# Causal select on GpSimd, exponent-bit rounding and a reordered opening in a four-layer gated-attention kernel

## The reference, cut to what matters

```python
for l in range(4):
    x = x + tanh(g_xattn[l]) * attention[l](layernorm(x), ctx)
    x = x + tanh(g_ffn[l]) * ffn[l](layernorm(x))
# attention 2: a query sees the keys up to its own place
scores = einsum('bhqd,bhkd->bhqk', Q, K) / sqrt(8)
scores = where(tril(ones), scores, -inf)
attn = softmax(scores)
# ffn 3: blocks of 32 are divided by max|block| / 7.5, rounded to the grid
# +-(m/8, or (1+m/8)*2^(e-1)), 0..7.5, ties to the lower value, and multiplied back
out = quantised(x) @ quantised(weight).T + bias
```

## Time and profile before

| | |
|---|---|
| three runs | 963.58, 964.5, 966.36 us; median 964.5 |
| the profiled execution | 962.56 us, its span 960.8 us |
| mean granted TensorE clock | 0.963 of full speed |
| TensorE busy | 883.2 us, 92% |
| VectorE / ScalarE / GpSimd busy | 74% / 66% / 48% |

### The profile page before, as it was taken

How to read it: one execution, slowest core, us unless ns; L and a number is a source line. 1 busy time by engine, 2 the same in 40 slices (tenths; PEclk the granted TensorE clock), 3 DMA queues, 4 the chain that set the end, 5 groups by cost and what they waited for, 6 DMA issues and landing times.

```text
span 960.8 us, 22930 instructions
## 1 busy us (share of the span) xinstructions
PE 883.2 (92%) x8153; PEld 614.4 (64%) x8153; DVE 707.6 (74%) x2203; ACT 638.1 (66%) x1463; POOL 457.2 (48%) x563
## 2 busy tenths in 40 slices
PE   4797889999999999999987899999999999999973
PEld 2343446866799987478443365767679987887432
DVE  4898997768452378987998999798754257747987
ACT  1587667676876436796664777777787557777751
POOL 5527554862851134545356265555642514612362
PEclk7799999999999999999998999999999999999975
DMA  6523242221110010002102020120110100000000
GB/s 161 127 59 100 53 121 53 77 64 37 28 45 1 17 34 3 20 26 65 33 20 73 20 71 23 36 53 19 37 36 1 30 23 18 14 23 2 21 2 23
DMA packets 67664, 40.06 MB, mean 42 GB/s; under 512 B 8279, under 2 KB 65520, under 8 KB 67552
## 3 DMA queue, kind: packets, MB, share of 16 engines
q1 hardware_dynamic: 61056, 28.93, 11.6%
q0 software_dynamic: 2208, 6.78, 2.6%
q10 hardware_dynamic: 4288, 2.87, 1.3%
HBM read 11.19 MB, written 1.05 MB: 13 GB/s over the span
## 4 chain that ended last, share of the span: by engine, by line
PE 74%; DVE 11%; ACT 5%; POOL 5%; issue 3%; DMA 2%; ACTq 1%; SPq 0%; DVEq 0%; POOLq 0%
PE banks L1065 13%; PE banks L1056 13%; PE banks L889 9%; PE banks L1025 7%; PE banks L865 5%; PE banks L842 5%; PE banks L828 4%; PE banks L1035 4%; DVE mx L1372 3%; PE banks L821 3%; POOL h L596 3%; PE banks L994 2%; ACT probs L735 2%; PE banks L934 2%; PE banks L850 1%
## 5 line engine op out<-in xcount | busy, mean ns | idle before, releaser
L1372 DVE TENSOR_REDUCE mx<-banks 128x4 f32<-128x1024 f32 (+1 forms) x240 | 284.3, 1217 | 29.6 <-PE banks L842 22.1
L735 ACT ACTIVATE probs<-banks 128x512 f32<-128x512 f32 (+1 forms) x512 | 258.3, 581 | 55.1 <-PE banks L865 35.7
L793 ACT ACTIVATE probs<-banks,b_sb 128x256 f32<-128x256 f32 x288 | 117.4, 472 | 71.4 <-PE banks L1056 69.8
L889 PE MATMUL banks<-probs,v_aug 128*9 128x256 f32 (+1 forms) x2048 | 151.1, 378 | 7.2 <-ACT probs L735 6.3
L589 POOL TENSOR_TENSOR rstd<-veps,mhalf 128x2 f32<-128x2 f32 x64 | 46.2, 722 | 197.9 <-DVE veps L1321 197.2
L1065 PE MATMUL banks<-w_sb,probs 128*128 128x128 f32 x1152 | 139.9, 276 | 0.0
L1065 PEld LDWEIGHTS banks<-w_sb,probs 128*128 128x128 f32 x1152 | 135.6, 192 | 4.7 <-issue 2.1
L1056 PE MATMUL banks<-hT,w_sb 128*128 128x256 f32 x576 | 137.1, 382 | 0.0
L637 POOL TENSOR_TENSOR rn<-ss,mhalf 128x32 f32<-128x32 f32 x16 | 87.9, 5497 | 77.8 <-DVE ss L1168 77.8
L1056 PEld LDWEIGHTS banks<-hT,w_sb 128*128 128x128 f32 x576 | 104.3, 190 | 13.6 <-issue 0.8
L1244 DVE SCALAR_TENSOR_TENSOR xs<-banks,comb,xs 128x128 f32<-128x128 f32 x144 | 43.7, 345 | 91.9 <-PE banks L1065 87.2
(11 more groups left out here) (203 smaller groups left out, 1476.8 us busy)
## 6 DMA issues: line engine op xcount, KB each, us to landing
k_st<-k_parts SPq DMA_DIRECT2D x186, 64.0 KB, 2.0
q_st<-q_parts SPq DMA_DIRECT2D x186, 64.0 KB, 2.1
w_sb<-in_w POOLq DMA_DIRECT2D x16, 256.0 KB, 3.4
fc_sb<-in_fc POOLq DMA_DIRECT2D x6, 256.0 KB, 3.9
x_in<-in_x SPq DMA_DIRECT2D x8, 128.0 KB, 3.6
cT<-in_ctxT SPq DMA_DIRECT2D x8, 128.0 KB, 3.1
out_x<-xs SPq DMA_DIRECT2D x8, 128.0 KB, 1.9
q_st<-mT SPq DMA_DIRECT2D x32, 16.0 KB
```

Source lines behind the costliest of these rows:

```text
L735: nc.scalar.activation(probs[s][:, part % UNIT_RING, 2 * a:2 * a + 2, 0:n], b_bank(w, a + 1)[:, 0:2 * n].rearrange("p (j q) -> p j q", j=2 ...
L793: ins = nc.scalar.activation(hid[s][:, part % UNIT_RING, c, :], b_bank(w, half + 1)[:, j * ROWS:(j + 1) * ROWS], ACT.Gelu, bias=b1_sb[:, p ...
L889: ins = nc.tensor.matmul(c_bank(b, l, u // 4)[VW * i:VW * i + VR, g % 2, q0:ROWS], v_aug[s][:, t, 4 * g + i, :], probs[s][:, u % UNIT_RING ...
L1372: nc.vector.tensor_reduce(mx[s][:, r, :, hp0:hp0 + n], banks[:, first:first + 2, :].rearrange("p a (n k) -> p a n k", n=n), AX.X, ALU.max) ...
```

## The change

1. **Causal mask of the turned scores.** The four matmuls of each unit (L870 to L878) go. GpSimd gets one `affine_select` per unit on `probs`, in place, over four heads times the 128 queries of the diagonal block, after the exponentials; `weigh` waits for it. The row-wise mask (L850) stays. `ckq`, its load and its cast go.
2. **Rounding.** Part 4 takes the exponent bits of y with a bitwise and on VectorE, in place of ScalarE's square; eight parts (4 to 11) with one VectorE instruction each follow the division, then the multiplication back as part 12.
3. **Opening.** VectorE clears slot 0 first, makes the first statistics, then copies the weights by heads; slot 3 is cleared after the first norm. ScalarE evaluates one tanh on one element ahead of everything and the gates after the first keys. Of the `attention_loads`, two small ones are issued by ScalarE at the start, the three large ones by SyncE after the second tile of maxima of stream 0. K's first-term moves of streams 0 and 1 go to SyncE's queue. The `setup` parts stand among the maxima of stream 0 (places 4, 7, 9, 11). `late_loads` move from step 50 to 80.
4. **Order.** `TURNS_TAKEN` and `BANKS_TAKEN` are new. Stream 0's query now comes before stream 1's keys, stream 0's maxima before stream 2's norm. In layer 2 the mean distance between a unit's `attend` and its `weigh` is 12.2 steps where it was 10.3; elsewhere the order of the steps is close to the former one.

```diff
-MAGIC = 1.5 * 2.0 ** 23
+MAGIC = 1.5 * 2.0 ** 20
+EXPONENT = 0x7F800000
-ROW_PARTS, KEY_ROW_PARTS, FP6_PARTS, ... = 5, 3, 14, 4, 4
+ROW_PARTS, KEY_ROW_PARTS, FP6_PARTS, ... = 5, 3, 13, 4, 4
-BLK_AT, ..., LATE_AT = 90, 110, 9, 230, 12, 50
+BLK_AT, ..., LATE_AT = 90, 110, 9, 230, 12, 80
...
# stream_steps
-        out += [("setup", 0, part) for part in range(SETUP_PARTS)] * (l == 0)
+        if l == 0:
+            for part, place in enumerate((4, 7, 9, 11)):
+                tiles.insert(place, ("setup", 0, part))
...
# sync
-                    if b >= SPLIT_STREAMS or l > 0:
+                    if step == "keys" or b >= SPLIT_STREAMS or l > 0:
...
+                if (step, b, l, part) == ("maxima", 0, 0, 1):
+                    for dst, src in attention_loads[EARLY_LOADS:]:
+                        sp.dma_start(dst, src).then_inc(attn_loaded, 16)
...
# gpsimd
+                if step == "attend" and l == CAUSAL:
+                    pool.wait_ge(sems["b_read"], w.at("b_read", 2))
+                    seen = probs[s][:, part % UNIT_RING, :, 0:P]
+                    nc.gpsimd.affine_select(seen, seen, [[0, 4], [1, P]], ALU.is_ge, 0.0, base=0, channel_multiplier=-1)\
+                        .then_inc(sems["causal_ready"], 1)
...
# scalar
+            for dst, src in attention_loads[:EARLY_LOADS]:
+                act.dma_start(dst, src).then_inc(attn_loaded, 16)
+            act.wait_ge(zeros_ready, 1)
+            nc.scalar.activation(warm[:, :], mhalf[0:1, 0:1], ACT.Tanh)
...
-                    if b < SPLIT_STREAMS and l == 0:
+                    if step == "query" and b < SPLIT_STREAMS and l == 0:
...
-                if step == "query" and (b, l) == (0, 0):
+                if (step, b, l) == ("keys", 0, 0):
                     act.wait_ge(gates_loaded, 16 * len(gate_loads))
                     nc.scalar.activation(tg[:, :], gates[:, :], ACT.Tanh).then_inc(gates_done, 1)
...
-                if step == "quantise" and part == 4:
-                    nc.scalar.activation(work_rows[1][s][:, :, :], work_rows[0][s][:, :, :], ACT.Square)\
...
# tensor: the mask's matmuls in scores_turned go; weigh:
+                if l == CAUSAL:
+                    pe.wait_ge(sems["causal_ready"], w.at_step("causal_ready", 1, "attend", b, l, u))
+                else:
+                    pe.wait_ge(sems["b_read"], w.at_step("b_read", 2, "attend", b, l, u))
...
# vector
+            clear_keys(nc.vector, 0, cleared_dve)
-            dve.wait_ge(weights_loaded, 16 * len(weight_loads))
-            split_heads(0).then_inc(first_ready, 1)
...
                 if part == 4:
+                    return nc.vector.tensor_scalar(a.bitcast(U32), y.bitcast(U32), EXPONENT, None, ALU.bitwise_and)
                 if part == 5:
+                    return nc.vector.tensor_scalar(m2, a, 1.0, MAGIC, ALU.max, ALU.mult)
                 if part == 6:
+                    return nc.vector.tensor_tensor(inv, y, m2, ALU.add)
                 if part == 7:
+                    return nc.vector.tensor_tensor(inv, inv, m2, ALU.subtract)
                 if part == 8:
+                    return nc.vector.tensor_tensor(y, inv, y, ALU.subtract)
                 if part == 9:
+                    return nc.vector.scalar_tensor_tensor(a, y, 16.0 * MAGIC, m2, ALU.mult, ALU.is_ge)
                 if part == 10:
+                    return nc.vector.tensor_tensor(a, a, m2, ALU.mult)
                 if part == 11:
+                    return nc.vector.scalar_tensor_tensor(y, a, -0.125 / MAGIC, inv, ALU.mult, ALU.add)
...
                     if (b, l) == (0, 0):
-                        clear_keys(nc.vector, 0, cleared_dve)
-                        clear_queries(nc.vector, 3)
-                        clear_keys(nc.vector, 3, cleared_dve)
+                        dve.wait_ge(weights_loaded, 16 * len(weight_loads))
+                        split_heads(0).then_inc(first_ready, 1)
...
+                    if b == 0:
+                        clear_queries(nc.vector, 3)
+                        clear_keys(nc.vector, 3, cleared_dve)
```

More of the change, by code:

```diff
@@ L351, in flamingo @@
         ident = sb("ident", [P, P])
-        mask_b = sb("mask_b", [P, 3, P], BF16)
-        mask_swapped = sb("mask_swapped", [P, 3, P], BF16)
-        identb, cqk_b, ckq_b = (mask_b[:, i, :] for i in range(3))
+        mask_b = sb("mask_b", [P, 2, P], BF16)
+        mask_swapped = sb("mask_swapped", [P, 2, P], BF16)
+        identb, cqk_b = (mask_b[:, i, :] for i in range(2))
         before = sb("before", [P, RT, ROWS], BF16)
@@ L425, in flamingo @@
         before_f = spare[:, 2 * D:6 * D].rearrange("p (t k) -> p t k", t=RT)
-        cqk, ckq = (spare[:, i * D:(i + 1) * D] for i in range(2))
+        cqk = spare[:, 0:D]
         w3_sb = work_rows[0][0][:, 1, :]
@@ L697, in _ @@
                                          bias=bcol[:, l, c:c + 1]).then_inc(sems["b_read"], 1)
-                    if b < SPLIT_STREAMS and l == 0:
-                        name, terms, st = ("k", K_TERMS, k_st[s]) if step == "keys" else ("q", Q_TERMS, q_st[s])
+                    if step == "query" and b < SPLIT_STREAMS and l == 0:
                         act.wait_ge(*CLEARED[s])
                         act.wait_ge(sems[f"hi_ready{s}"], w.at(f"hi_ready{s}", 1))
-                        move_parts(act, terms, 0, st, parts[s], sems[f"{name}_moved{s}"])
-                if step == "query" and (b, l) == (0, 0):
+                        move_parts(act, Q_TERMS, 0, q_st[s], parts[s], sems[f"q_moved{s}"])
+                if (step, b, l) == ("keys", 0, 0):
                     act.wait_ge(gates_loaded, 16 * len(gate_loads))
                     nc.scalar.activation(tg[:, :], gates[:, :], ACT.Tanh).then_inc(gates_done, 1)
-                    for dst, src in attention_loads[:EARLY_LOADS]:
-                        act.dma_start(dst, src).then_inc(attn_loaded, 16)
-                if (step, b, l) == ("keys", 1, 0) and STEP["keys", 1, 0, 0] < STEP["setup", 0, 0, 0]:
-                    for dst, src in attention_loads[EARLY_LOADS:]:
-                        act.dma_start(dst, src).then_inc(attn_loaded, 16)
                 if w.i == LATE_AT:
@@ L1503, in _ @@
                     accumulate(s, lambda r: comb[s][:, r, part:part + 1])
-                if step == "quantise" and part not in (3, 4, FP6_PARTS - 1):
+                if step == "quantise" and part not in (3, FP6_PARTS - 1):
                     if part == 0:
                         dve.wait_ge(sems[f"h_ready{s}"], w.at_step(f"h_ready{s}", 1, "norm", b, 2 * LAYERS - 1, 0))
-                    elif part == 5:
-                        dve.wait_ge(sems["fp6_squared"], w.at_step("fp6_squared", 1, "quantise", b, l, 4))
+                    elif part == 4:
+                        dve.wait_ge(sems["fp6_divided"], w.at_step("fp6_divided", 1, "quantise", b, l, 3))
                     else:
```

132 lines of the change are left out of this document (52 added, 80 removed).

## The result

The changed kernel takes 959.43 us (median of 22 runs, 954.34 to 964.91) where the kernel before took 964.36 beside it (22 runs): ratio 0.9955, 95% interval 0.9943 to 0.9966. It is faster, by 4.9 us between the medians and 4.3 us by the ratio; 18 were forecast. The time lies inside the range given, 933 to 960, by 0.6 us.

What follows compares the result with a forecast made beforehand. Limits differed: TensorE in masked stretches, VectorE from 24 to 120 and 470 to 560 us, nothing full in the first 24. Gains 6.1 + 7.5 + 2 + 2.5 = 18.1 us gave 946.4 us, range 933 to 960.

Steps and rivals of the forecast that it cites:

- the pricing of the new order at nothing: Order of steps: no term of its own in the sum, only more steps between `attend` and `weigh`, 12.2 against 10.3.
- the opening: First 24 us: first scores at about 16 us, nine earlier, of which 7.5 us gained, ends 3 and 10.
- rounding and end: Rounding of streams 0 to 2, 2 us, ends 0 and 4.8; last stream's end, 2.5 us, ends 1 and 3.5.
- the mask: Layer 2's masked stretches: TensorE loses 13.9 us of work, selects cost GpSimd 1.0 us each; 6.1 us gained.
- (a): Masked waves: GpSimd late with a select at 1.34 us, opening at its lower end; 956.5, up to 964.5 us; 15%.
- (d): Opening: comes no earlier because first scores wait for a landing as now; 10.6 us gained, 953.9 us; 10%.
- case (c): Mask: select as cheap as a copy, TensorE's whole 13.9 us come back; 25.8 us gained in all, 938.7 us; 20%.
- The arithmetic of GpSimd's capacity: Masked waves: GpSimd's work summed per window; mask gains 13.8 us at 0.7 us a select, loses 4.0 at 1.34.
- The wait behind the norm: GpSimd's queue: 12.2 steps cover 1 us of latency, not a select behind a 5.45 us norm of heads; no size given.
- Rival (b): Masked waves: slower, select costs 3.25 us like a per-partition tensor_scalar; 66 us more, 1031 us; 9%.
- The prediction's measure: Opening: VectorE's idle time before 24 us counts; 12.3 us falls to 6 with scores at 16 us.
- the prediction's own last check: Opening: if first scores come at 16 us but VectorE idles as much before 60 us, the shift was absorbed.

Runs made afterwards that it cites:

- the two variants: Kernel before with the GpSimd select alone, ratio 1.0428; and all parts of the change with the select, former order after step 40, ratio 1.0453.
- the opening alone: Kernel before with the reordered start of every queue and the new steps up to stream 0's first attend, mask and rounding as before: ratio 0.9985.
- doubled selects: Changed kernel with every select of the probabilities issued twice in a row: ratio 1.0081 to the kernel before.

## Why the prediction was wrong

**The failed step is the pricing of the new order at nothing, and with it the sum itself.** The forecast took four terms, each read from the kernel before, and added them as if the order of steps were given. Measured in the former order, where they were read, they are worth far less: the opening 6.1 us less than its term, rounding and end 4.0, the mask 2.1 even with a select that costs nothing, and together they give 4.9 of the 18.1. In the new order they are worth about what was forecast or more, but there they only make up for an order that loses 20 us without them. That the time lies inside the range is no merit of the sum: it lies 0.6 us from the upper end, which was set by rivals (a) and (d).

| term | forecast, us | former order | new order |
|---|---|---|---|
| opening | 7.5 | 1.4 | 5.4 |
| mask by select | 6.1 | 4.0 (no select at all) | 8.7 |
| rounding and end | 4.5 | 0.5 | 14 to 15 |
| new order, former parts | 0 | | -20 |
| the select, against no select | (in the mask's) | -45 to -49 | 0 |
| together, measured | 18.1 | 4.9 without the select | 4.3 |

The new order's column adds up to 8 or 9, not 4.3. Its errors, about 2 us for each term, may cover that, and parts that are taken out one at a time need not add up: opening and rounding are 19.7 to 20.3 us one by one and 16.0 together. With the 16.0 the column closes: -20.3 + 16.0 + 8.7 = 4.4. Why the new order loses 20 us under the former ones was not tried further, and stays open.

**Mask.** The amount removed was right to the row: 64 units, 0.217 us. The select was priced at 1.0 us and takes 0.64; the bound from the nearest one-input rows was the better guide. By the Trainium skill's GPSIMD Engine Reference ("Performance pitfalls for Q7 kernels") the estimate was 0.44 or 0.87 us plus dispatch; the 64 selects lie between the two at 0.64, and nothing here shows the branching price of 5.1 us that its cycle accounting would give. What failed is case (c)'s condition, a cheap select, as the thing that decides. It holds, and still less than half of 13.8 us came in the former order. The windows showed TensorE at 99% of these stretches, and I took that for a distance to the next limit. It is none: of the 13.9 us taken away 4.0 came in the former order and 8.7 in the new one, and then other waits hold the time. Of these only VectorE's maxima were tried, 3.1 us for half of their work in layer 2. Rival (a) had the number, 956.5 and up to 964.5, and not the mechanism: its select of 1.34 us would hold up the waves, and here TensorE waits 2.6 us for all selects. The arithmetic of GpSimd's capacity came near in size and by another road: for 1.34 us a select it gave 17.8 us more than for a cheap one, and 1.28 us measured 12 more. It went by the sums of whole windows, while in the trace the sum of the first wave fits (35.1 of 40 us) and the queueing sits in its last ten microseconds.

**The wait behind the norm.** The prediction named it: 12.2 steps cover a select, "not a select that stands behind the 5.45 us of a norm of heads". It was not priced. In the new order it does not strike (TensorE's longest wait for a select is 0.7 us); in the former order it is half of 41 us. Rival (b) had the right sign for that case and the wrong mechanism: a time of over 1000 us (1005.6 and 1008.1 in the two variants) needs no slow select, only a fast one in a bad place.

**Opening.** First scores at 16.28 us against 16: right. Worth 5.4 us against 7.5 in the new order: within its ends of 3 and 10. In the former order it is 1.4. The prediction's measure, how much of VectorE's idle time goes, fits both. The first 60 us of the kernel before, of the opening alone in the former order, and of the changed kernel:

```profile
0.00:60.00 60.00, 39.09 (x322) 18.64 (x322) 44.87 (x95) 28.68 (x66) 25.05 (x46) 0.80 0.47 121
0.00:60.00 60.00, 42.93 (x335) 20.41 (x335) 46.27 (x97) 29.96 (x69) 24.07 (x45) 0.74 0.45 117
0.00:60.00 60.00, 45.17 (x387) 21.62 (x388) 51.04 (x106) 33.55 (x77) 26.30 (x48) 0.83 0.43 116
```

VectorE idles 15.1, 13.7 and 9.0 us. The other traces agree: 13.8 to 16.1 us with the former opening, in either order; 15.6 and 15.7 with the new opening in the former order; 9.1 to 11.2 with both new. Stream 0's attention ends at 61.6 to 63.8 us in the first group, at 61.2 to 63.2 in the second and at 56.4 to 58.6 in the third. So in the former order the lead of 7.4 us at the first scores is all but gone by 60 us, and in the new order some 5 of 8.6 us stay. The shift was absorbed in the former order, as the prediction's own last check describes. One place is in the chains of all three traces of the second group: ScalarE issues `late_loads` ahead of an exponential that TensorE waits for (1.0 to 2.1 us). In the opening alone:

```profile
51.21 0.48 ACT raw L744
...
51.73 0.46 ACTq L715
...
52.21 0.51 ACTq L715
...
52.77 0.61 ACT probs L737
```

Most of the lead is lost before that, and by what is open: TensorE's first `weigh` comes at 40.8 us where it came at 42.2 before and comes at 37.3 in the changed kernel. The granted clock does not decide it. In the opening alone it is 0.50, the 1.2 GHz level, from 32 to 40 us; but the kernel before has 0.50 from 24 to 32 us, and the variant with all parts and no mask in the former order, which has 1.00 up to 32 us, ends stream 0's attention no earlier, at 63.1. Rival (d), an opening that does not come earlier, is refuted in its premise.

**Rounding and end.** 2 + 2.5 were forecast, and the former order gives 0.5, within the end of 0 for the first term and below the end of 1 for the second. ScalarE's step is gone. The end is 4.6 us against 3.5. No step of another stream stands between the eight instructions; the first three take 0.70, 0.59 and 0.72 us where 0.29, 0.29 and 0.43 were counted, 1.0 us more, while GpSimd multiplies back the streams before (from 941.74 to 943.78 us), and the five behind it take 0.42 or 0.43. That the same part is worth 14 us in the new order lay outside every bound.

## What to carry to other kernels

With a static order of steps, a part's worth belongs to the part and the order together: price a change of order by what it leaves room for, and never add terms read in the old order. "99% busy" says which engine ends last, not how far behind the next one is; what is taken from it pays only down to that next limit. A short instruction put into the chain of every unit can cost what stands ahead of it in its engine's queue, here 45 us (against the same kernel without it) for 64 instructions of 0.64. And a single trace can be 5 us ahead of another with the same code: compare ratios of many runs, and let a trace say only where.

## What the runs showed of the hardware that was not expected

- A select with an affine condition on GpSimd takes 0.64 us for 128x512 float32 in place (64 of them, 624 to 827 ns), no more than a two-input operation on half as many elements (0.67 us).
- GpSimd's power of 128x32 elements takes 5.45 us, the product of the same tile 0.30: eighteen times as much for sixteen such calls, and yet the kernel before is not faster without them (1.0017).
- The granted clock differs between single runs of the same instructions: from 16 to 24 us it was 0.50 in the opening alone and 1.00 in the variant with all parts and no mask in the former order, with nearly the same work of TensorE there (6.4 and 6.6 us); from 120 to 130 us it was 1.00 in the changed kernel and 0.66 in the one with doubled selects, which differ only later.
- VectorE's rounding instructions of 128x256 took 0.59 to 0.72 us while GpSimd worked beside them at the end of the changed kernel, and 0.42 or 0.43 right after. Two forms are mixed in this, and the overlap was not tried apart.
